# Second layer routed by halves of tokens, seven expert tiles woven into the second attention

## What is computed

```
xn = layernorm(x)
# attention: RMS-normalised rows, q and k normalised over the 256 tokens, softmax over the 16 x 16 products of each head
q, k, v = split(rms(xn) @ w_qkv.T);  q, k = l2norm(q), l2norm(k);  attn = softmax(exp(temperature) * q k^T)
s = (attn v) @ w_out.T
# experts: 4 experts, each token goes to 2
p = softmax(gelu(xn @ rW1 + rb1) @ rW2 + rb2);  w, idx = top_k(p, 2)
g = sum over the token's experts e of  w_e * (gelu(xn @ We1[e] + be1[e]) @ We2[e] + be2[e])
x = x + s * silu(g)
```

## Time and profile before

| what | us |
|---|---|
| median of 3 runs (890.62 to 894.91) | 893.07 |
| the profiled execution | 892.01 |
| its span, first to last instruction | 889.9 |
| PE busy | 730.4 |
| DVE busy | 565.2 |
| ACT busy | 485.7 |
| POOL busy | 452.1 |
| mean granted TensorE clock | 0.911 |

### The profile page before, as it was taken

One profiled execution on the slowest core, in us unless ns is written; L12 is line 12 of the kernel. 1 busy time (PEld: TensorE's weight loads), 2 busy tenths in 40 slices (PEclk: granted clock), 3 DMA queues, 4 the chain that ended last, 5 costly groups with the idle time before them and its releaser, 6 DMA issues. The chain is left out here.

```text
span 889.9 us, 17097 instructions
## 1 busy us (share of the span) xinstructions
PE 730.4 (82%) x5338; PEld 496.8 (56%) x5338; DVE 565.2 (64%) x1276; ACT 485.7 (55%) x919; POOL 452.1 (51%) x398
## 2 busy tenths in 40 slices
PE   0977786879898999967999889899988578999960
PEld 0751231223232333336999888798877467989950
DVE  7768889888888898831333376657364474333446
ACT  0752563557777787863445538568721144545521
POOL 7911553558888999831555444400044652445440
PEclk9997796789999999997999999999986589999995
DMA  8994451113222322138776786440001411777739
GB/s 252 314 281 150 154 157 48 29 50 101 69 89 69 101 86 73 52 103 243 224 217 221 231 256 205 151 122 1 1 27 34 155 37 46 229 225 207 223 95 247
DMA packets 112254, 124.06 MB, mean 139 GB/s; under 512 B 10560, under 2 KB 93168, under 8 KB 112208
## 3 DMA queue, kind: packets, MB, share of 16 engines
q1 hardware_dynamic: 104080, 106.71, 40.2%
q0 software_dynamic: 8128, 16.78, 5.3%
HBM read 82.50 MB, written 40.81 MB: 139 GB/s over the span
## 5 line engine op out<-in xcount | busy, mean ns | idle before, releaser
L665 POOL DMA_INDIRECT yg_dram<-work x138 | 135.0, 978 | 176.1 <-DVE work L1703 133.4
L1238 ACT ACTIVATE work<-wide,work 128x256 f32<-128x256 f32 x324 | 130.2, 474 | 113.0 <-PE wide L877 112.1
L1596 DVE TENSOR_REDUCE work<-wide 128x4 bf16<-128x1024 f32 x128 | 156.8, 1226 | 29.7 <-PE wide L756 22.9
L888 PE MATMUL wide<-work 128*128 128x128 f32 x1296 | 161.0, 279 | 0.0
L888 PEld LDWEIGHTS wide<-work 128*128 128x128 f32 x1296 | 154.9, 195 | 0.8 <-ACT work L1238 0.2
L877 PE MATMUL wide<-xT,work 128*128 128x256 f32 x552 | 134.4, 387 | 11.6 <-issue 9.2
L877 PEld LDWEIGHTS wide<-xT,work 128*128 128x128 f32 x552 | 100.7, 193 | 26.5 <-issue 13.9
L629 POOL TENSOR_TENSOR work<-work,biasT 128x1024 f32<-128x1024 f32 x32 | 75.7, 2365 | 76.2 <-ACT work L1176 75.8
L629 POOL TENSOR_TENSOR yy<-yy,biasT 128x1024 f32<-128x1024 f32 x32 | 75.8, 2370 | 28.5 <-ACT yy L1176 27.9
L1183 ACT ACTIVATE yy<-yy 128x1024 f32<-128x1024 f32 x64 | 67.4, 1054 | 40.9 <-DVE yy L1605 37.7
L750 PE MATMUL wide<-biasA,turnb 128*128 128x512 bf16 x256 | 85.2, 417 | 3.8 <-ACT bufC L1111 3.0
(11 more groups left out here) (280 smaller groups left out, 1201.4 us busy)
## 6 DMA issues: line engine op xcount, KB each, us to landing
work<-in_wcat SPq DMA_DIRECT2D x73, 578.0 KB
work<-stk_dram SPq DMA_DIRECT2D x128, 96.0 KB
xg_dram<-empty SPq DMA_DIRECT2D x35, 260.0 KB, 2.8
work<-xg_dram SPq DMA_DIRECT2D x69, 130.0 KB
yy<-yg_dram SPq DMA_DIRECT2D x14, 512.0 KB, 6.6
stk_dram<-yy SPq DMA_DIRECT2D x16, 384.0 KB, 2.9
stk_dram<-yy SPq DMA_DIRECT2D x16, 256.0 KB, 3.1
biasT<-ext_dram SPq DMA_DIRECT2D x1, 3072.0 KB, 14.9
```

What stands on the lines that cost most here:

```text
L665: g.indirect_dma_start(out=yg_dram[l], out_offset=bass.IndirectOffsetOnAxis(ap=yid[v][:, s_:s_ + 1].bitcast(u32), axis=0), in_=yb[u][:, s_ ...
L888: last = mm(YP[u][:, s_ * D:(s_ + 1) * D], hb[u][:, c, s_ * P:(s_ + 1) * P], wb[v][:, HID + c * D:HID + (c + 1) * D], start=(c == 0), stop ...
L1238: A(hb[u][:, c, :], bank[2 + 2 * u + c // 2][:, (c % 2) * TS:(c % 2 + 1) * TS], ACT.Gelu, bias=wb[v][:, bc:bc + 1]).then_inc(m["gelu"], 1)
L1596: V.tensor_reduce(nmax[:, :, 2 * place(t):2 * place(t) + 2].rearrange("p c e -> p e c"), wide[t % 2][:, :].rearrange("p (e c k) -> p e c k ...
```

## The change

The second layer's routing is split by halves of tokens: token tiles 6 to 15, then 16 to 31. The first half's choice, counts and slots come on DVE before the second half's logits, with a sort of tiles that leaves for the first NFULL = 7 tiles rows of the first half alone. POOL scatters the first half's 20 pieces, then the second half's 32, with the stores of tiles 0 to 3 put between them. The attention's 40 slots are no longer one run: four slots (BEFORE) come first, then for each of the seven tiles up, two slots, down, two slots, the next tile's transposes, one slot. To make room in PSUM the woven tiles use banks 0 to 2 singly and the attention banks 3 to 7, some of which it had doubled before. The 22 other tiles follow. Results of the first half (two quarters) are fetched beside tiles 16 to 19 and added beside tiles 22 and 24; the last fetch has four DMAs. Steps of ACT and DVE for these tiles are written out, not looped. In the diff's new functions `choose_second`, `count_second`, `tiles_second`, `slots_second` and `rows_second` do for one half what the `route_` functions did for all.

```diff
+NJB = tiles_for(E1, (TA - TD) * P)
+NFULL = -(-((TA - TD) * P * TOPK - E1 * (TS - 1)) // TS)
+ROUTED1 = ((TD, TA), (TA, T))
+PART = E1 * TA
+LOOPED = (-(-NJA // NWB), NJ1 // NWB)
...
+BEFORE = 4
+STORED = 4
+STORE_BEHIND = {10: 0, 16: 1, 22: 2, 28: 3}
+
+
+def slots_behind(j, part):
+
+    per = [2, 2, 1]
+    at = BEFORE + j * sum(per) + sum(per[0:part])
+    return range(at, NSLOT2 if j == NFULL - 1 and part == 2 else at + per[part])
...
-                    sp.wait_ge(rou[1]["scattered"], 16 * TOPK * (HEAD1 - TD))
-                    sp.wait_ge(rou[1]["tail"], 16 * TOPK * (T - HEAD1))
+                    sp.wait_ge(rou[1]["scattered"], 16 * TOPK * (TA - TD))
...
+                    if l and j == NFULL:
+                        sp.wait_ge(rou[1]["routed"], 2)
+                        load_weights(j, j % NWB)
+                        sp.wait_ge(rou[1]["tail"], 16 * TOPK * (T - TA))
+                        load_rows(j, j % 2)
+                    else:
+                        load(j, j % NWB)
+                    if l and j == NJB + 3:
+                        sp.wait_ge(com[1]["dense"], 1)
+                        stored_through(NJB)
+                    if l and NJB + 3 <= j < NJB + 7:
+                        fetch((j - NJB - 3) // 2, (j - NJB - 3) % 2)
...
-                    for q in range(4):
+                    for q in range(2, 4):
...
             def scatter_second():
+                pool.wait_ge(pre[1]["xs"], NB // 2)
+                pool.wait_ge(rou[1]["kept"], 1)
+                mark_choice(1, 0, TD, TA)
+                pool.wait_ge(s_xgz[1], NEMPTY[1] * 16)
+                pool.wait_ge(rou[1]["slots"], 1)
+                for t in range(TD, TA):
+                    scatter_rows(1, 0, t)
+                pool.wait_ge(rou[1]["slots"], 2)
+                pool.wait_ge(rou[1]["scattered"], 16 * (TA - TD))
+                mark_choice(1, 1, TD, TA)
+                for t in range(TD, TA):
+                    scatter_rows(1, 1, t)
                 pool.wait_ge(pre[1]["xs"], NB)
-                pool.wait_ge(rou[1]["kept"], 1)
-                mark_choice(1, 0, TD, T)
-                pool.wait_ge(s_xgz[1], NEMPTY[1] * 16)
-                n = 0
+                pool.wait_ge(rou[1]["kept"], 2)
+                mark_choice(1, 0, TA, T)
+                sent = 0
                 for k in range(TOPK):
-                    pool.wait_ge(rou[1]["slots"], k + 1)
-                    for lo, hi, landed in ((TD, HEAD1, "scattered"), (HEAD1, T, "tail")):
-                        if k:
-                            pool.wait_ge(rou[1][landed], 16 * (hi - lo))
-                            mark_choice(1, 1, lo, hi)
-                        for t in range(lo, hi):
-                            follow_second_attention(n)
-                            scatter_rows(1, k, t, landed)
-                            n += 1
-
-            def follow_second_attention(n):
-                half = T - FIRST[1]
-                if n < half and n >= LEAD and n % 2 == 0:
-                    pool.wait_ge(A1["nns"], 2 + min(NB, n - LEAD + 2))
-                elif n >= half + LEAD and n % 2 == 0:
-                    pool.wait_ge(A1["s"], 1 + min(NB, (n - half - LEAD) * 3 // 4 + 1))
+                    pool.wait_ge(rou[1]["slots"], 3 + k)
+                    if k:
+                        pool.wait_ge(rou[1]["tail"], 16 * (T - TA))
+                        mark_choice(1, 1, TA, T)
+                    for t in range(TA, T):
+                        scatter_rows(1, k, t, "tail")
+                        sent += 1
+                        if sent in STORE_BEHIND:
+                            store_output(1, STORE_BEHIND[sent], STORE_BEHIND[sent])
...
+            pe.wait_ge(rou[1]["kept"], 1)
             for j in (NDA, NDA + 1):
                 up_rows(m, j, j % NWB, xTd[j // E1])
             down_rows(m, NDA, NDA % NWB)
-            route_pe(1, E1, bank[0], bank[1])
+            route_pe_second(1, bank[0], bank[1])
             down_rows(m, NDA + 1, (NDA + 1) % NWB)
-            pe.wait_ge(rou[1]["kept"], 1)
+            pe.wait_ge(rou[1]["kept"], 2)
+            pe.wait_ge(m["gelu"], NDJ * 4 + 8)
+            pe.wait_ge(m["y"], NDJ + 4)
...
+            def transposes_between(j):
+                pe.wait_ge(m[f"xg{j % 2}"], j // 2 * 16 + 16)
+                pe.wait_ge(m["xT"], j + 2)
+                pe.wait_ge(m["y"], j + DENSE[1] + 4)
+                tr(bank[0][:, 0:P], xg[j % 2][:, 0, 0:D], ident[:, :])
+                tr(bank[0][:, P:2 * P], xg[j % 2][:, 1, 0:D], ident[:, :]).then_inc(m["T"], 1)
+
+            def up_between(j):
+                pe.wait_ge(m[f"W{j % NWB}"], j // NWB * 16 + 32)
+                pe.wait_ge(m["xT"], j + 3)
+                up_rows(m, j + DENSE[1], j % NWB, xT[j % 2][:, :], bank[1:3])
+
+            for i in range(BEFORE):
+                attention_slot(i)
+            transposes_between(0)
+            for j in range(NFULL):
+                up_between(j)
+                for i in slots_behind(j, 0):
+                    attention_slot(i)
+                down_rows(m, j + DENSE[1], j % NWB, bank[0][:, TS:2 * TS])
+                for i in slots_behind(j, 1):
+                    attention_slot(i)
+                if j + 1 < NFULL:
+                    transposes_between(j + 1)
+                for i in slots_behind(j, 2):
+                    attention_slot(i)
             pe.wait_ge(a["s"], NB + 1)
             experts(1, NJ1)
...
+            for i in range(NB // 2, NB + 2):
+                for stage, lag in ((normalised, 0), (transposed_again, 1), (hidden, 2)):
+                    if NB // 2 <= i - lag < NB:
+                        stage(i - lag, (i - lag) % 2)
+                if i == NB // 2 + 1:
+                    route_act_second(0)
+            route_act_second(1)
...
+                gelus(moe[1], j + DENSE[1], j % NWB, j // NWB * 16 + 32, bank[1:3])
+                for part in range(3):
+                    for i in slots_behind(j, part):
+                        attention_slot(i)
...
+            def second_experts(nj):
+                copy_rows, outputs = row_copier(1), output_writer(1)
+                for j in range(NFULL, NFULL + 2):
+                    copy_rows(j, j % NWB, j // 2)
+                for j in range(NFULL, nj):
+                    if j + 2 < nj:
+                        copy_rows(j + 2, (j + 2) % NWB, (j + 2) // 2)
+                    outputs(j, j % NWB, j // 2)
+                    if NFULL < j <= NFULL + E1:
+                        weigh_dense(j - NFULL - 1)
+                    elif j in (NJB + 9, NJB + 11):
+                        add_choices(1, (j - NJB - 9) // 2)
...
             finish_half(1, com[0]["x1"])
+            router_logits(0)
+            choose_second(0)
             keep_dense(8)
             keep_dense(9)
-            router_logits(0)
...
+            count_second(0, bank[2][:, 0:PART], bank[2][:, PART:2 * PART])
+            tiles_second(0)
+            slots_second(0)
+            rows_second(0)
             router_logits(1)
-            route_shift(1)
-            route_probabilities(1)
-            for k in range(TOPK):
-                route_choose(1, k)
-            route_weights(1)
-            route_keep_counts(1, bank[0], bank[1])
-            route_tiles(1)
-            route_offsets(1)
-            route_slots(1)
+            choose_second(1)
             keep_dense(NDA)
             keep_dense(NDA + 1)
-
+            count_second(1, bank[0], bank[1])
+            tiles_second(1)
+            slots_second(1)
...
+            copy_rows, outputs = row_copier(1), output_writer(1)
+            for i in range(BEFORE):
+                attention_slot(i)
+            copy_rows(0, 0, 0, bank[0])
+            for j in range(NFULL):
+                for i in slots_behind(j, 0):
+                    attention_slot(i)
+                outputs(j, j % NWB, j // 2, bank[0][:, TS:2 * TS])
+                for i in slots_behind(j, 1):
+                    attention_slot(i)
+                if j + 1 < NFULL:
+                    copy_rows(j + 1, (j + 1) % NWB, (j + 1) // 2, bank[0])
+                for i in slots_behind(j, 2):
+                    attention_slot(i)
+            second_experts(NJ1)
```

549 lines of the change are left out of this document (311 added, 238 removed).

## The result

The changed kernel takes 906.35 us (median of 900.58 to 908.17) against 891.85 us before (885.0 to 894.91): a ratio of 1.0163, 95% interval 1.0119 to 1.0207. I had put 891 with a range of 875 to 906, so it is slower by 14.5 us where I expected no change, and just outside the range. The profiled execution is the quickest of the four, 900.58 us with a span of 897.7.

The account below looks back on a forecast made before the run. PE was taken to bound the expert tiles and the attention's first part, DVE its second. Start 671.5, woven stretch 91.6 + 11, tiles 86.9 + 2, tail 26.7 gave a span of 889.7, time 891, range 875 to 906.

Parts of the forecast that it names:

- Which delays PE's router matmuls by some 2.9 us: Router stage: two table loads of 1.28 us for the first half's exponential delay PE's matmuls by 2.9 us.
- The first woven tile starts at 671.5: Start of weaving, after scatters and row loads: 671.5 us, bounds 668 and 676, slots 2 and 3 ending near 667.
- Woven stretch 91.6 + 11 = 102.6: Second attention with seven tiles: 91.6 us at full clock plus 11 for gaps and lower clock, bounds 4 and 22.
- the walk: Step-by-step full-clock estimate of the woven stretch: 0.9 + 31.7 first part, 5 roots, 54 second part.
- Second-part tiles at 13 us: Attention's second part: one tile with five slots takes 13 us, against 13.9 simply added; GELUs begin near 1.1 us.
- Rival C: Second part: PE falls to the lower clock after each wait for an exponential, giving 904; chance 0.17.
- 22 tiles, 86.9 + 2: Plain tiles after the attention: 22 x 3.95 = 86.9 us, plus 2 for early fetches delaying row loads.
- Tail 26.7: After the last matmul: 26.7 us instead of 30.2, since fewer results remain to fetch.
- Rival B: Woven stretch: tiles fill the gaps and PE stays at full clock, giving 878 (872 to 885); chance 0.27.
- D: Rival: GpSimd's queue, stores between scatters, binds the woven tiles, +8 to 899; chance 0.10.
- E: Rival: each ScalarE table switch also costs a 1.38 us drain, +5.5 to +10, 897 to 901; chance 0.05.
- 21 us are lost: Second attention of the kernel before: 93 us against 71.7 at full clock, lost to lower clock and unexplained gaps.

Follow-up runs that it names:

- r2: Kernel before plus one unused exponential on ScalarE inside the router stage, bringing two table loads: ratio 1.0148.
- r13: Kernel before plus an unused exponential and GELU, the same two table loads, ahead of the router stage in ScalarE's idle time: ratio 1.0004.
- r14: Changed kernel with nothing woven, plus five unread matmuls in PE's two waits of the router stage: ratio 0.9974.
- r6: Changed kernel plus 64 idle semaphore increments on VectorE ahead of the third and fourth dense tile: ratio 1.0226.
- r5: Changed kernel with the first half's router exponential a plain copy, plus 64 idle increments on VectorE: ratio 1.0138.
- r8: Changed kernel, still routed by halves, but all 40 slots first and no tile woven: ratio 1.0016 over its quicker eight, 1.008 over all twelve times.
- r1: Changed kernel with the first half's router exponential a plain copy, so no table load in the router stage: ratio 1.0157.
- r11: Changed kernel, all seven tiles woven, with the first half's exponential moved ahead of the router stage: ratio 1.0132.
- r15: The changed kernel measured again, not altered: ratio 1.0165.
- r9: Changed kernel with nothing woven and the first half's exponential moved ahead of the router stage: ratio 0.9963.
- r17: Unwoven kernel with the early exponential (r9), its second attention given back two banks per step: ratio 0.9897.
- r3: Changed kernel plus five unread matmuls in PE's two waits of the router stage: ratio 1.0183.
- r18: Changed kernel with the early exponential, eleven slots ahead of the first woven tile and only two tiles woven: ratio 1.0174.
- r7: Kernel before plus 64 idle increments on VectorE: ratio 0.9989.

## Why the prediction was wrong, step by step

- **"Which delays PE's router matmuls by some 2.9 us"**: this step failed. The delay itself is about right (1.21 + 1.02 us of waits), but I took PE's rate as given. The stage took 32 us instead of 17 since the clock fell to 1.2 GHz and stayed there; r2, r13 and r14 show the cause. Its price in the whole, measured on F, is 6 to 8 us (r6 to r5) or 11 (r8's two groups, where no tile is woven), not 15. On S it is not measured: r2 added 1.5% to the kernel before, r1 took nothing off the changed one.
- **Routing on DVE (+4.9)**: right, 620.58 to 625.46. **Scatters**: 1.26 us each, right; SP issued the row loads at 670.23.
- **"The first woven tile starts at 671.5"**, bounds 668 to 676: 676.98. It was not the rows that came last but slots 2 and 3, which I put near 667 and which waited for the second half's route until 674.40. DVE's steps for it began at 667.16 where I had 655.5: behind the slow stage PE's down product ended only at 661.95, and DVE began another 5.2 us after it. Neither alone makes the tile late: without the loads (r1, where DVE idles 5.6 us at the same step) it begins at 670.31, and without the hole it would be near 672, my estimate from 676.98 less 5.2.
- **Woven stretch 91.6 + 11 = 102.6**: 109.0, so the term for gaps and the lower level was 17.4 and not 11. Most of it lies in the first part: three tiles took 14.8, 17.9 and 12.9, 45.6 us against 32.6 by the walk (0.9 + 31.7). In r11, on F, they took 12.0, 10.6 and 10.1, 32.7, so the walk was right for a kernel without holes; the changed kernel's trace has two on DVE there, L2010 at 688.51 and at 700.84, 3.4 and 4.4 us after their last inputs (PE's L1085 ends at 685.1 and 696.5), and lower-clock matmuls behind the second (3.55 us for the down product at 703.43). From the fourth tile to the first plain one it is 63.4 us in both, against 59 by the walk. **Second-part tiles at 13 us** was thus the other failed step: the last three took 16.0, 16.2 and 17.5, in r11 15.8, 14.5 and 19.1. I had the GELUs "begun near 1.1", that is with their table in place; the load comes behind their wait, so they began 2.4 us after the up product did, the exponential was later by as much, and the down product ran at the lower clock in the changed kernel (3.26 us). Rival C, priced at 904 for a fall of the clock after such waits, came nearest to the time, but in part by luck: its mechanism is not general, as in r11 the same wait of 2.93 us is followed by a down product at the full clock (1.95 us at 732.35), and the waits cost by themselves.
- **22 tiles, 86.9 + 2**: 87.1 (786.02 to 873.1); the early fetches cost nothing that shows against the 2 us that I gave them. **Tail 26.7**: 24.6 (873.1 to 897.7).
- Sum against the forecast of 889.7: +5.5 start, +6.4 woven stretch, -1.8 tiles, -2.1 tail, 897.7. The other 5.8 us up to the median are executions slower than the profiled one, and the miss of the range hangs on them; r15's profile (span 909.5) has 114.4 us for the woven stretch.
- **Rival B** (tiles fill the gaps) is refuted by r9 and r11, **D** by the trace (between 676 and 786 POOL's stores wait for DVE's outputs, 52.8 us in all, and no output waits for a store), **E** too. By the Trainium skill, "ScalarE: Activation LUTs", section "What ACT_TABLE_LOAD costs", a drain follows the load; here the GELUs follow at once (755.21 + 1.28, 756.51).
- **"21 us are lost"** ahead of the tiles, the room that the change was to use, was no property of the kernel. On kind F the kernel before ends its last slot near 701 (r13, the kernel before with two loads more), 61 us after the first begins, and then PE stands until tile 0's scattered rows have come (POOL's last scatter begins at 709.14, SP loads the rows at 711.49):

```profile
713.79 0.45 PE L899 MATMUL wide<-ident,work 128*128 128x128 f32 x1 [12.63 <-issue]
```

There routing by halves has something to win. r17 begins its first plain tile at 712.62, without that wait, though its first slot begins 7 us later than r13's; that is 1.2 us sooner, and from there to the end it takes 138.5 us against 142.4, where the early fetches stand. On kind S no unwoven variant was measured.

## What to carry to other kernels

Before a table switch is put beside matmuls, look who waits for that ScalarE instruction: two loads of 1.28 us cost 0.9 to 1.5% inside a run of small matmuls and nothing ahead of it, in ACT's idle time, and five idle matmuls in the pauses were as good on F. Look where the table load stands against the waits of the activation that needs it: where it carries them, a dummy activation ahead takes it off the path. Interleave two stages only where the second one's inputs are there: a tile that stands in PE's queue ahead of its rows holds every slot behind it, and routing early pays without any weaving.

## What the hardware showed that I had not expected

- PE's clock stayed at the lower level through 25 us of back-to-back router matmuls (29 us busy of 32, clock 0.60), and came back only afterwards. The same program seems to keep or lose it from run to run (r8's two groups of times).
- A table load for the exponential went ahead of its activation's wait (in r18 the load at 713.63, the exponential at 729.59), one for GELU stood behind it (755.21 above).
- On kind S, DVE and ACT began some steps 3 to 6 us after their inputs with nothing that the trace shows in the way (r1 above; in r3 DVE's L2013 at 682.01 had its product at 676.2; in the changed kernel L1951 at 667.16; in the kernel before ACT's L1313 at 730.66 had its product at 728.0, and behind it stands the wait of 1.85 us at 731.08 in the earlier trace rows); on kind F I found none. In r1 and r3 such holes stood where the router's gain should have shown. The kernel before's second attention takes 93 us on S and 61 on F; how much of that is such holes is not measured. What the engines wait for there stays open: r5 to r7 were to test the code's position and fell on F. Until it is known, a difference of 1 to 2% on S can be the place of these holes as well as the change.
